# A two-step top-p graph kernel: the second step's band end, its 8 strip segments with 4 rounds, and one reversed pass for equal values

## The reference, cut to what matters

```python
def _top_p_attention(X, W1, W2, W3):
    q = X @ W1.T @ W2.T
    k = X @ W3.T
    probs = jax.nn.softmax(q @ k.T / TAU, axis=-1)
    idx = jnp.argsort(-probs, axis=-1)
    sp = jnp.take_along_axis(probs, idx, axis=-1)
    cs = jnp.cumsum(sp, axis=-1)
    keep_sorted = cs - sp < TOP_P                 # TOP_P = 0.9
    mask = jnp.zeros(probs.shape, dtype=bool).at[rows, idx].set(keep_sorted)
    A = probs * mask
    return A / jnp.maximum(A.sum(-1, keepdims=True), 1e-12)

for n in range(2):                                # two steps
    A = _top_p_attention(Xa, W1, W2, W3)
    Xf = R @ Xf
    Xa = A @ Xa
    Z = Z + Xf @ U1[n].T + Xa @ U2[n].T
```

## Time and profile before

| what | before |
|---|---|
| device time, median of 3 runs | 886.03 us (885.93 to 888.31) |
| span of the profiled execution, first to last instruction | 869.3 us |
| time around the span (median less span) | 16.7 us |
| mean granted TensorE clock | 0.936 |
| DVE busy | 661.3 us (76%) |
| PE busy | 743.8 us (86%) |
| ACT busy | 484.1 us (56%) |
| POOL busy | 273.4 us (31%) |

### The profile page before, as it was taken

One profiled execution on the slowest core, in us unless ns is written; L12 is line 12 of the kernel. 1 busy time (PEld: TensorE's weight loads), 2 busy tenths in 40 slices (PEclk: granted clock), 3 DMA queues, 4 the chain that ended last, 5 costly groups with the idle time before them and its releaser, 6 DMA issues.

```text
span 869.3 us, 15803 instructions
## 1 busy us (share of the span) xinstructions
PE 743.8 (86%) x5226; PEld 536.3 (62%) x5226; DVE 661.3 (76%) x2281; ACT 484.1 (56%) x723; POOL 273.4 (31%) x584
## 2 busy tenths in 40 slices
PE   3999999768999878999999987878778797798894
PEld 2455555427999634677778676655446675786563
DVE  6658686843444377899872699999898999999757
ACT  5777676414555326555563484668686675822153
POOL 3401412335666400211200052041341577770000
PEclk9999999997999899999999999788988898989897
DMA  8674100055888500000000000000000001101001
GB/s 149 104 119 67 38 7 20 26 158 163 236 231 235 156 14 0 2 1 2 2 1 1 2 2 2 2 1 2 1 0 2 2 1 56 43 2 32 1 1 49
DMA packets 47368, 41.95 MB, mean 48 GB/s; under 512 B 7376, under 2 KB 44112, under 8 KB 47280
## 3 DMA queue, kind: packets, MB, share of 16 engines
q1 hardware_dynamic: 29488, 19.95, 8.3%
q0 software_dynamic: 11456, 14.62, 8.2%
q10 hardware_dynamic: 6336, 6.32, 2.9%
HBM read 39.69 MB, written 9.57 MB: 57 GB/s over the span
## 4 chain that ended last, share of the span: by engine, by line
DVE 20%; PE 17%; issue 15%; POOLq 4%; ACT 4%; POOL 3%; DVEq 0%; ACTq 0%
PE bank L2148 4%; DVE big L1605 4%; PE bank L2131 3%; PE bank L2052 3%; DVE cand L1523 2%; DVE cand L1369 2%; DVE hacc L1518 2%; PE bank L2332 2%; PE bank L2345 1%; ACT big L1878 1%; DVE rm L1363 1%; ACT big L1848 1%; PE bank L295 1%; POOLq L1238 1%; DVE cand L1544 1%
## 5 line engine op out<-in xcount | busy, mean ns | idle before, releaser
L2131 PE MATMUL bank<-ident,big 128*128 128x128 f32 x512 | 81.5, 309 | 27.1 <-DVEq L1628 18.6
L1878 ACT ACTIVATE big<-bank 128x512 f32<-128x512 f32 x128 | 71.0, 597 | 49.9 <-PE bank L2131 48.7
L2131 PEld LDWEIGHTS bank<-ident,big 128*128 128x128 f32 x512 | 62.5, 156 | 54.8 <-ACT big L1878 20.4
L2052 PE MATMUL bank<-kk,qq 64*128 64x512 f32 x256 | 76.0, 710 | 17.0 <-ACT big L1848 16.4
L1848 ACT ACTIVATE big<-bank,negm 128x2048 f32<-128x2048 f32 x32 | 62.6, 1958 | 46.0 <-DVE fsc L1655 35.7
L2059 PEld LDWEIGHTS bank<-parts,adjT 128*128 128x128 bf16 x1536 | 86.6, 98 | 2.4 <-issue 2.1
L2059 PE MATMUL bank<-parts,adjT 128*128 128x128 bf16 x1536 | 87.9, 219 | 0.0
L1605 DVE SCALAR_TENSOR_TENSOR big<-big,st 128x2048 f32<-128x2048 f32 x32 | 73.9, 2347 | 3.3 <-PE bank L2131 3.3
L403 POOL DMA_INDIRECT ys_scratch<-big,parts x62 | 59.9, 967 | 32.6 <-ACT big L758 22.8
L848 PE MATMUL bank<-big,xn 128*128 128x512 f32 x128 | 62.2, 608 | 5.7 <-DVE big L550 5.7
L832 PE MATMUL bank<-xnT 128*128 128x512 f32 x128 | 62.4, 612 | 2.3 <-DVE xnT L539 2.3
(11 more groups left out here) (382 smaller groups left out, 1549.5 us busy)
## 6 DMA issues: line engine op xcount, KB each, us to landing
big<-in_L_ffn_w_dram SPq DMA_DIRECT2D x93, 128.0 KB
big<-in_adj_dram POOLq DMA_DIRECT2D x8, 512.0 KB, 7.6
big<-xs_scratch ACTq DMA_DIRECT2D x31, 132.0 KB, 2.9
kk<-in_adj_dram POOLq DMA_DIRECT2D x4, 512.0 KB, 8.2
qq<-in_adj_dram POOLq DMA_DIRECT2D x4, 512.0 KB, 10.0
xs_scratch<-hacc SPq DMA_DIRECT2D x9, 132.0 KB
xs_scratch<-hacc ACTq DMA_DIRECT2D x8, 132.0 KB
res<-in_x_dram SPq DMA_DIRECT2D x4, 256.0 KB, 6.9
```

The lines of the kernel that those rows point to most:

```text
L1878: nc.scalar.activation(MT[:, 4 * q:4 * q + 4, s * P:(s + 1) * P], bank[:, 5 + q % 2, :].rearrange("p (j i) -> p j i", j=4), ACT.Copy).then ...
L2052: nc.tensor.matmul(bank[:, c, :], qq[lo:lo + DA, (g * G + s) * P:(g * G + s + 1) * P], kk[lo:lo + DA, c * CH:(c + 1) * CH], start=True, st ...
L2131: mm = nc.tensor.transpose(bank[:, 5 + q % 2, j * P:(j + 1) * P], mk[:, s, jt * P:(jt + 1) * P], ident[:, :])
```

## The change

In the second step (the first is untouched but for the names of sizes):

- The 2048 columns are cut into 8 segments in place of 16. A segment is no longer one run of columns but four runs of 64, one from each quarter of the row (`strips`), 256 columns in all. There are 64 candidates a tile in place of 128, in `cand[:, b]` as in the first step.
- 4 rounds in place of 5, so 32 values in order in place of 40 (`R8`).
- The count in the right half and the second row of needles go; one reversed `match_replace` of 2048 columns for each tile takes the place of two of 1024.
- POOL computes the second threshold and the band end from other formulas that use the counts at both probes: `after_first` has 12 instructions for g > 0 in place of 8 with as many drains, `after_second` has 11 as before with one drain fewer.

Its core:

```diff
-        NSEG = (8, 16)
-        ROUNDS = (4, 5)
+        NSEG = 8
+        ROUNDS = 4
+        STRIPS = 4
-        SLOPE = 0.7
-        REACH = 40.0
+        JUMP = (1.23, 9.05, 0.476)
+        STEP = (1.0 / 0.823, 32.84, 38.66, 1.663)
@@ after_first
                     if g:
                         nc.gpsimd.tensor_scalar(B(B_Y, s), B(B_S1, s), float(N), 0.5 * 2.0 ** FIRST, ALU.add, ALU.mult)
+                        nc.gpsimd.tensor_scalar(B(B_C, s), B(B_S1, s), -0.5, 0.5 * N + JUMP[2], ALU.mult, ALU.add)
...
                     nc.gpsimd.tensor_tensor(B(B_B, s), B(B_Y, s), B(B_R1, s), ALU.subtract)
-                    nc.gpsimd.tensor_scalar(B(B_TG, s), BI(B_TG, s), 1.0 / SLOPE, None, ALU.mult)
+                    nc.gpsimd.tensor_scalar(BI(B_C, s), BI(B_C, s), -1.0, 2.0 * ONE, ALU.mult, ALU.add)
+                    nc.gpsimd.tensor_scalar(B(B_TG, s), BI(B_TG, s), 1.0, None, ALU.mult)
                     pool.drain()
-                    nc.gpsimd.tensor_scalar(B(B_U, s), BI(B_B, s), -1.0 / SLOPE, ONE + FIRST * OCTAVE, ALU.mult, ALU.add)
+                    nc.gpsimd.tensor_scalar(B(B_U, s), BI(B_B, s), -1.0, B(B_TG, s), ALU.mult, ALU.add)
+                    nc.gpsimd.tensor_scalar(B(B_C, s), B(B_C, s), JUMP[1], JUMP[0], ALU.mult, ALU.add)
+                    nc.gpsimd.tensor_scalar(B(B_W, s), B(B_TG, s), STEP[0], None, ALU.mult)
                     pool.drain()
-                    nc.gpsimd.tensor_tensor(B(B_U, s), B(B_U, s), B(B_TG, s), ALU.add)
+                    nc.gpsimd.tensor_scalar(B(B_U, s), B(B_U, s), B(B_C, s), ONE + FIRST * OCTAVE, ALU.mult, ALU.add)
@@ after_second
                     if g:
-                        nc.gpsimd.tensor_scalar(B(B_C, s), B(B_S2, s), float(N), 0.5, ALU.add, ALU.mult)
+                        nc.gpsimd.tensor_scalar(B(B_Y, s), B(B_S2, s), float(N), 0.5, ALU.add, ALU.mult)
+                        nc.gpsimd.tensor_scalar(B(B_C, s), B(B_S2, s), -0.5, 0.5 * N + STEP[3], ALU.mult, ALU.add)
...
-                    nc.gpsimd.tensor_scalar(B(B_C, s), B(B_C, s), REACH * OCTAVE, None, ALU.mult)
+                    nc.gpsimd.tensor_tensor(B(B_W, s), B(B_W, s), B(B_C, s), ALU.mult)
                     pool.drain()
-                    nc.gpsimd.tensor_tensor(B(B_TG, s), B(B_TG, s), B(B_C, s), ALU.add)
-                    pool.drain()
-                    nc.gpsimd.tensor_tensor(B(B_U, s), B(B_U, s), B(B_TG, s), ALU.add)
+                    nc.gpsimd.tensor_tensor(B(B_U, s), B(B_U, s), B(B_W, s), ALU.add)
                     pool.drain()
@@ group
-                    R8 = 8 * ROUNDS[n]
-                    SEG = N // NSEG[n]
-                    cg = cand1 if n else cand[:, b, :, :]
+                    R8 = 8 * ROUNDS
+                    cg = cand[:, b, :, :]
...
-                            for j in range(NSEG[n]):
-                                vc = op(nc.vector.max(cg[:, s, 8 * j:8 * j + 8], lowg[:, j * SEG:(j + 1) * SEG]))
+                            strips = lowg.rearrange("p (a j n) -> p j a n", a=STRIPS, j=NSEG)
+                            for j in range(NSEG):
+                                vc = op(nc.vector.max(cg[:, s, 8 * j:8 * j + 8], strips[:, j, :, :]))
...
-                        for s in range(G):
-                            w = op(nc.vector.tensor_scalar(cand2[:, s, 0:64], cg[:, s, 64:128], S1(V_, s), None,
-                                                           ALU.is_equal, ALU.add, accum_out=S1(MH, s)))
                         since(v)
-                        e = [op(nc.vector.tensor_scalar(eq8[:, 1, s, :], iota8[:, :], S1(EX, s), S1(V_, s), ALU.is_lt,
-                                                        ALU.mult)) for s in range(G)]
-                        since(w)
-                        v = op(nc.vector.tensor_tensor(S(DH), S(EX), S(MH), ALU.subtract))
-                        since(v)
-                        f = [op(nc.vector.tensor_scalar(eq8[:, 0, s, :], iota8[:, :], S1(DH, s), S1(V_, s), ALU.is_lt,
+                        e = [op(nc.vector.tensor_scalar(eq8[:, s, :], iota8[:, :], S1(EX, s), S1(V_, s), ALU.is_lt,
                                                         ALU.mult)) for s in range(G)]
                         for s in range(G):
                             since(e[s])
-                            op(nc.vector.match_replace(mk[:, s, :N // 2 - 1:-1], eq8[:, 1, s, :],
-                                                       prob[:, b, s, :N // 2 - 1:-1], 0.0))
-                            since(f[s])
-                            e[s] = op(nc.vector.match_replace(mk[:, s, N // 2 - 1::-1], eq8[:, 0, s, :],
-                                                              prob[:, b, s, N // 2 - 1::-1], 0.0))
+                            e[s] = op(nc.vector.match_replace(mk[:, s, ::-1], eq8[:, s, :], prob[:, b, s, ::-1], 0.0))
```

More of the change, by code:

```diff
@@ L1047, in tries @@
             return 4 + 8 * (g - 1) + 2 * (2 * k + s) if g else 2 * s + k
-        tv = sb("tv", [P, G, 8 * max(ROUNDS)])
+        tv = sb("tv", [P, G, 8 * ROUNDS])
         cand = sb("cand", [P, 2, G, 64])
-        cand1 = cand[:, :, :, :].rearrange("p b s n -> p (b s n)").rearrange("p (s n) -> p s n", s=G)
-        top = sb("top", [P, G, 8 * max(ROUNDS)])
-        cum = sb("cum", [P, G, 8 * max(ROUNDS)])
+        top = sb("top", [P, G, 8 * ROUNDS])
+        cum = sb("cum", [P, G, 8 * ROUNDS])
         rm8 = sb("rm8", [P, 8])
@@ L1057, in build @@
         st = sb("st", [P, 16, G])
-        (T_, TB, F_, GE, Q_, FH, V_, SM, LO, HI, THETA, EX, EM, MH, DH) = range(15)
-        bt = sb("bt", [P, 13, G])
-        (B_R1, B_S1, B_R2, B_S2, B_T2, B_TB, B_TB1, B_TG, B_Y, B_B, B_C, B_U, B_V) = range(13)
+        (T_, TB, F_, GE, Q_, FH, V_, SM, LO, HI, THETA, EX, EM) = range(13)
+        bt = sb("bt", [P, 14, G])
+        (B_R1, B_S1, B_R2, B_S2, B_T2, B_TB, B_TB1, B_TG, B_Y, B_B, B_C, B_U, B_V, B_W) = range(14)
         first = sb("first", [P, 1])
         fl = sb("fl", [P, 2 * G])
-        eq8 = sb("eq8", [P, 2, G, 8])
+        eq8 = sb("eq8", [P, G, 8])
         iota8 = sb("iota8", [P, 8])
-        cand2 = sb("cand2", [P, G, 128])
+        cand2 = sb("cand2", [P, G, 64])
         fsc = sb("fsc", [P, 2, G])
@@ L1206, in after_first @@
                         nc.gpsimd.tensor_scalar(B(B_Y, s), B(B_S1, s), 2.0 ** FIRST, None, ALU.mult)
+                        nc.gpsimd.tensor_scalar(B(B_C, s), B(B_S1, s), -1.0, N + JUMP[2], ALU.mult, ALU.add)
                     nc.gpsimd.tensor_scalar(B(B_TG, s), Z[:, b, s:s + 1], 1.0 - TOP_P, None, ALU.mult)
@@ L1223, in after_second @@
                     if g:
-                        nc.gpsimd.tensor_scalar(B(B_C, s), B(B_S2, s), float(N), 0.5, ALU.add, ALU.mult)
+                        nc.gpsimd.tensor_scalar(B(B_Y, s), B(B_S2, s), float(N), 0.5, ALU.add, ALU.mult)
+                        nc.gpsimd.tensor_scalar(B(B_C, s), B(B_S2, s), -0.5, 0.5 * N + STEP[3], ALU.mult, ALU.add)
                     else:
                         pool.wait_ge(counted, 2 * s + 2)
-                        nc.gpsimd.tensor_scalar(B(B_C, s), B(B_S2, s), 1.0, None, ALU.mult)
@@ L1228, in after_second @@
-                    nc.gpsimd.tensor_tensor(B(B_TG, s), B(B_TG, s), B(B_V, s), ALU.add)
+                        nc.gpsimd.tensor_scalar(B(B_Y, s), B(B_S2, s), 1.0, None, ALU.mult)
+                        nc.gpsimd.tensor_scalar(B(B_C, s), B(B_S2, s), -1.0, N + STEP[3], ALU.mult, ALU.add)
+                    nc.gpsimd.tensor_tensor(B(B_TG, s), B(B_W, s), B(B_V, s), ALU.add)
                     pool.drain()
-                    nc.gpsimd.tensor_tensor(B(B_Y, s), B(B_C, s), B(B_T2, s), ALU.mult)
@@ L1231, in after_second @@
-                    nc.gpsimd.tensor_scalar(B(B_C, s), B(B_C, s), -1.0, N + 0.5, ALU.mult, ALU.add)
+                    nc.gpsimd.tensor_tensor(B(B_Y, s), B(B_Y, s), B(B_T2, s), ALU.mult)
+                    nc.gpsimd.tensor_scalar(BI(B_C, s), BI(B_C, s), -1.0, 2.0 * ONE, ALU.mult, ALU.add)
                     pool.drain()
                     nc.gpsimd.tensor_tensor(B(B_B, s), B(B_Y, s), B(B_R2, s), ALU.subtract)
-                    nc.gpsimd.tensor_scalar(BI(B_C, s), BI(B_C, s), -1.0, 2.0 * ONE, ALU.mult, ALU.add)
+                    nc.gpsimd.tensor_scalar(B(B_W, s), B(B_C, s), STEP[2] * OCTAVE, STEP[1] * OCTAVE, ALU.mult, ALU.add)
@@ L1235, in after_second @@
                     pool.drain()
-                    nc.gpsimd.tensor_scalar(B(B_U, s), BI(B_B, s), -1.0 / SLOPE, None, ALU.mult)
-                    nc.gpsimd.tensor_scalar(B(B_C, s), B(B_C, s), REACH * OCTAVE, None, ALU.mult)
+                    nc.gpsimd.tensor_scalar(B(B_U, s), BI(B_B, s), -STEP[0], B(B_TG, s), ALU.mult, ALU.add)
+                    nc.gpsimd.tensor_tensor(B(B_W, s), B(B_W, s), B(B_C, s), ALU.mult)
                     pool.drain()
-                    nc.gpsimd.tensor_tensor(B(B_TG, s), B(B_TG, s), B(B_C, s), ALU.add)
@@ L1535, in group @@
                     got = [0] * G
-                    for r in range(ROUNDS[n]):
```

(3 more changed lines are left out.)

## The result

| what | before | after |
|---|---|---|
| device time, median of 4 runs each | 886.48 us (885.93 to 888.31) | 1708.84 us (1706.55 to 1710.92) |
| ratio, with its 95% interval | | 1.9284 [1.9238, 1.9331] |
| span of the profiled execution | 869.3 us | 1704.8 us |
| mean granted TensorE clock | 0.936 | 0.723 |

What follows compares the result with a forecast made beforehand. DVE was taken to bound groups 0, 1 and 4 to 7, an ACT and PE chain groups 2 and 3. Group gains and collision losses summed to -5.6 us: 886.0 becomes 880.4 us, range 865 to 889.

Steps and rivals of the forecast that it cites:

- Match passes: DVE, each group: two reversed passes of 2048 columns take 4.58 us for four of 1024 at 4.78, saving 0.20.
- Equal values: DVE, each group: four of eight instructions stay, 0.87 us for 1.73, saving 0.86.
- The band is cut too short: Rival, chance 0.03: with 32 values for 40 a row may miss its target, and exact runs 40 rounds, over 180 us.
- What DVE sheds: DVE, each group: shorter segments, rounds, equal values and match passes sum to 3.80 us, taken as 3.9.
- the rule that the prediction named for them: Strips on DVE: hops between runs of two or more adjacent words are free, so 0.46 us a tile is saved.
- The collision: DVE's earlier two-input pass holds POOL's after_first while ACT waits; groups 2 and 3 lose 2.3 and 1.9 us.
- POOL keeps clear enough: Rival, chance 0.20: holds of POOL cost ACT nothing; 18.8 us gained, 867.2 us.
- DVE alone bounds: Rival, chance 0.07: all 8 groups gain 3.9 us, 31.2 in all, giving 854.8 us.
- the savings are not what they seem: Rival, chance 0.09: strips and group 5 bring no gain, leaving 1.9 us, 884.1 us, no difference.
- The match pass holds POOL: Rival, chance 0.11: long match passes also shut out POOL, 2.26 us in groups 1 to 6, giving 891.7 us.
- forecast hold on tile 0: Group 6: tile 0's second threshold comes at +28.7, band end at +36.2, making the group 1.2 us longer.
- 16.7 around it: Whole kernel: 16.7 us of time taken around the 863.7 us span to reach 880.4.

Runs made afterwards that it cites:

- the kernel without its search: Changed kernel with the exact search's branch taken above 127 flagged rows in place of above 0, leaving some values wrong: 862.78 us, ratio 0.9916 to before.
- by halves: Changed kernel with equal values dropped by half rows again, each segment's four runs within one half: 862.38 us, ratio 0.9908; run again 865.14 us, 0.996.
- two rows of needles: Changed kernel with a second set of 8 needles and a second reversed pass over the whole row for each tile: 894.74 us, ratio 1.0103.
- the old band end: Kernel by halves, 32 values, with POOL's after_first and after_second as before the change: 1962.03 us, ratio 2.251.
- the kernel with the wait in groups 2 and 3: By halves, DVE's masked pass there waiting for POOL's second threshold of tile 1: 879.75 us, ratio 0.9930; run again 865.24 us, 0.9924.

## Why the prediction was wrong

**The step that failed** is the edit "Match passes" with "Equal values": "1024 more columns add 1.10 to a pass ... so two take 4.58". It was costed as columns and never as capacity. The two rows of needles that go away held 16 needles, the one that stays holds 8, and both numbers stood in the code (`iota8` and `eq8`, 8 wide). The right question was how many equal values a row may have to drop, and no timeline answers that. The sum left the fallback `exact` at zero for this edit, and its true term is 3 x 274 = 822 us. Against before that is 886.48 + 822 less the 7.5 of the rest, 1701; measured 1708.84. Most of the other 8 us lie behind the last search and in group 3: against the profile without the search, groups 2 and 4 are 274.3 and 274.4 us longer, the stretch from group 7's answer to the end 279.1, and group 3 2.2.

**The rival "The band is cut too short"** (0.03) had the right event, the search, and the wrong cause: by halves the same band needs no search, two rows of needles remove it, and by halves only the old band end brings a search, mostly in other groups (0, 3, 4 and 6). Its price, "over 180 us", counted the two passes of a round at 2.3 us; the rows show 6.1 us a round in place of 4.6, and 31 us of scans and passes behind the rounds. A range that reaches to a fallback must also ask how many groups it hits: one row out of 256 sends the whole group there.

**What DVE sheds: right.** Strips cost nothing over one run of 256 columns (2.71 us for 2.74), so the rule that the prediction named for them holds here.

**The collision: right in groups 1 to 5 and 7, in group 6 right by luck.** Group by group the forecast differs from the profile of the kernel without its search by 1.3 us at most, in the sum by 1.7 (-5.6 for -7.3). The largest miss is group 4, -4.8 for -3.5. The clock over it was 1.00, where before had 0.91: the logits took 1.99 us for 3.68, and the row maximum, which the forecast had waiting for them, started at +5.0 without a wait in place of +6.1. That is 1.0 of the 1.3 us, and it belongs to the two executions compared, not to the change. In group 6 the forecast hold on tile 0 did not take place and one on tile 1 gave the same end, so there the number is luck. All of this compares one profiled execution of each kernel; the whole, -7.5 us for -5.6, rests on all runs (the interval is -10.1 to -4.5). "POOL keeps clear enough" (18.8 us), "DVE alone bounds" (31.2) and "the savings are not what they seem" (1.9) are out by it. "The match pass holds POOL" is out as well: in the rows of group 2 above POOL starts `after_first` at 596.54, inside the second match pass (from 595.69), at its usual 0.19 us, and nothing long starts inside a match pass in any group. The Trainium skill (SBUF — State Buffer, Who interferes with whom) says that an instruction of DVE with two SBUF inputs contends with POOL's reads and one with a single SBUF input does not; both halves hold here, with 2.2 to 2.4 us in place of 0.19 for one instruction of POOL.

**What was not in the forecast: the clock in it.** The forecast took the start of `after_first` in group 3 as given, +19.1. It hangs on the clock of the logits at the group's start. In the profile of the kernel without its search these ran at the higher clock and the group was hit all the same, since the masked pass came at +21.6. By halves the pass comes at +22.7 with fast logits, and there the clock decides whether the group is hit at all.

**Of the needles** the Trainium skill (Vector Engine (DVE) Microarchitecture Reference, The match/index hardware and the swap-based sort pattern) states that exactly eight needle values are clocked in, which is the number on which this change falls. It also says that any streamed element equal to a needle is replaced. The runs speak against that: then one needle would drop every equal value, a row that is to keep some of them would miss them in its sum, and before would search, which it does not; nor would eight more needles change anything, and they take away three searches.

## What to carry to other kernels

When two passes with their own operands are merged into one, count what the operands can hold, not only the columns: eight needles of one value drop eight equal elements, as these runs show. Where a kernel has a fallback that is never taken, price one taking of it (here 274 us, a third of the kernel) and ask of every edit on its guard what values bring it on, since no trace of before can show it. And a two-input pass of DVE that is moved earlier shuts POOL out at a new place; look whose wait lies there.

## What the runs showed of the hardware that was not expected

**The clock over eight products decides a collision elsewhere.** By halves, group 3 was hit or free as its logits took 3.79 or 1.99 us. Why the clock differed is not seen: at the end of group 2 PE was idle for 5.01 us in the one and 5.30 us in the other, the granted clock behind that was 0.50 in both, and the eight transposes just ahead of the logits took 1.06 us in both.

The late probe itself leaves PE idle for longer, and the clock is low behind it. In group 2 of the kernel without search PE has no work for 5.28 us, and the two products behind that run at half speed (granted clock 0.50 from 609.03 to 611.75):

```profile
609.03 2.08 PE L2106 MATMUL bank<-xnT,ident 128*128 128x512 f32 x2 [5.28 <-ACT parts L1891]
```

Group 3 of the kernel by halves, where it escaped, has 1.13 us for the same two (granted clock 1.00):

```profile
644.64 1.13 PE L2119 MATMUL bank<-xnT,ident 128*128 128x512 f32 x2 [2.66 <-ACT parts L1904]
```

Before has most of this already: 2.88 us idle, and 1.79 us for the two. Against it PE starts again 2.11 us later in the group (+33.9 for +31.8) and the answer of the flags comes 2.42 us later, so the clock adds some 0.3 us to what the wait for POOL costs.

**The sessions differ by 15 us, ahead of the second step and where DMA is busy.** The kernel before took 870.23, 871.79 and 885.31 us in the three sessions, each on a chip of its own; whether the chip or the session makes the difference can't be told apart. The second step starts 521 to 526 us after the start of the span in the four profiles of the session at 885, and at 505 to 509 in those of the other sessions without a search in group 0. The same stage in the kernel before as first profiled, and in the kernel with the wait in groups 2 and 3, from the slower session, by windows:

```profile
180.00:240.00 60.00, 50.02 (x280) 39.99 (x278) 23.67 (x114) 22.92 (x57) 36.71 (x49) 0.91 0.73 205
```

```profile
180.00:240.00 60.00, 46.10 (x253) 35.06 (x253) 22.90 (x103) 19.46 (x49) 32.59 (x45) 0.91 0.63 183
```

183 GB/s for 205, and 253 matrix products for 280 in the same 60 us. That DMA is the cause was not tested. In the later profiled executions the device time was 1.7 to 1.8 us above the span; the "16.7 around it" of the prediction was no overhead, but a span of 869.3 that fits the faster sessions (its second step starts at 506) beside a median of 886.03 that fits the slower one. That changed no term of the sum.
